# Two closing stages made one block, the chosen expert found inside the node stage, and the first four expert tiles taken singly

## What is computed

```python
H = gelu(layernorm(x) @ W1 + b1)              # 6250 x 1024
probs = softmax(H @ Wg + bg)                  # 6250 x 8
assign = argmax(probs)                        # the first largest
out = x + probs[assign] * (H @ Wd[assign] + bd[assign])
```

## Time and profile before

| | us |
|---|---|
| median of three runs | 2440.83 |
| the profiled execution | 2438.15 |
| its span in the trace | 2436.4 |
| busy: PE / DVE / POOL / ACT | 1969.0 / 1799.0 / 1456.7 / 869.7 |
| TensorE's mean granted clock | 0.902 |

### The profile page before, as it was taken

How to read it: one execution, slowest core, us unless ns; L and a number is a source line. 1 busy time by engine, 2 the same in 40 slices (tenths; PEclk the granted TensorE clock), 3 DMA queues, 4 the chain that set the end, 5 groups by cost and what they waited for, 6 DMA issues and landing times. The chain is left out here.

```text
span 2436.4 us, 50363 instructions
## 1 busy us (share of the span) xinstructions
PE 1969.0 (81%) x11356; PEld 1408.1 (58%) x11357; DVE 1799.0 (74%) x3100; ACT 869.7 (36%) x2796; POOL 1456.7 (60%) x1360
## 2 busy tenths in 40 slices
PE   8965777776777777777757999999889999679996
PEld 4533444554554544444545777777655555468885
DVE  6877999999999999999967888878776764321111
ACT  4532111111111111111116777777445555432221
POOL 4655777777777777777732777777654542023442
PEclk9987888888888888888878999999899999889998
DMA  6658999999999999999996888888534643464450
GB/s 218 222 177 275 359 362 358 361 360 354 360 362 355 363 356 359 358 358 360 349 231 205 304 277 278 280 278 277 170 130 169 219 159 119 172 232 168 154 186 36
DMA packets 388111, 649.78 MB, mean 267 GB/s; under 512 B 40235, under 2 KB 235951, under 8 KB 387925
## 3 DMA queue, kind: packets, MB, share of 16 engines
q1 hardware_dynamic: 200132, 277.43, 34.7%
q0 software_dynamic: 77824, 262.55, 30.2%
q10 hardware_dynamic: 110096, 109.07, 12.8%
HBM read 471.00 MB, written 178.83 MB: 267 GB/s over the span
## 5 line engine op out<-in xcount | busy, mean ns | idle before, releaser
L721 POOL DMA_INDIRECT s_kv<-kv_d,s_index x832 | 791.3, 951 | 266.0 <-issue 238.0
L1362 PE MATMUL a_sum_ps<-a_w,a_is_dst 128*128 128x260 f32 x1760 | 403.6, 388 | 20.5 <-DVE sums L1333 11.9
L1275 POOL TENSOR_TENSOR a_w<-a_v,a_w 128x512 f32<-128x512 f32 x220 | 299.1, 1365 | 164.8 <-ACT a_w L1232 107.5
L1362 PEld LDWEIGHTS a_sum_ps<-a_w,a_is_dst 128*128 128x128 f32 x1760 | 328.2, 191 | 95.8 <-issue 25.1
L867 PE MATMUL s_q_ps<-q,s_is_dst 128*128 x2496 | 366.9, 304 | 10.0 <-DVE s_key L776 8.7
L820 PE MATMUL s_mv_ps<-s_mixed 128*128 128x128 f32 x416 | 106.4, 436 | 272.2 <-DVE s_mixed L756 272.2
L771 DVE TENSOR_TENSOR s_key<-s_kv,s_rel_ps 128x1024 f32<-128x1024 f32 x208 | 253.3, 1218 | 63.0 <-issue 36.4
L867 PEld LDWEIGHTS s_q_ps<-q,s_is_dst 128*128 128x128 bf16 x2496 | 253.3, 107 | 79.2 <-issue 12.7
L1248 ACT ACTIVATE a_w<-a_v,a_w 128x64 f32<-128x64 f32 x1100 | 285.8, 335 | 3.5 <-DMA a_v<-v_d 3.5
L1309 DVE SCALAR_TENSOR_TENSOR a_is_dst<-node_of,first_node,a_col_ps 128x256 f32<-128x256 f32 x440 | 208.8, 475 | 82.7 <-PE a_sum_ps L1362 64.9
L781 DVE TENSOR_REDUCE s_part<-s_key 128x16 f32<-128x1024 f32 x208 | 253.7, 1220 | 10.7
(11 more groups left out here) (310 smaller groups left out, 2941.4 us busy)
## 6 DMA issues: line engine op xcount, KB each, us to landing
a_v<-v_d SPq DMA_DIRECT2D x440, 256.0 KB, 3.7
v_d<-s_kv ACTq DMA_DIRECT2D x208, 512.0 KB
s_local<-local_d SPq DMA_DIRECT2D x106, 256.0 KB, 6.0
xh_d<-h_hid SPq DMA_DIRECT2D x24, 1024.0 KB, 7.5
s_kind<-type_d SPq DMA_DIRECT2D x212, 64.0 KB, 6.6
s_kv<-kv_d,s_index POOLq DMA_INDIRECT x832
kv_d<-pkv SPq DMA_DIRECT2D x50, 256.0 KB, 2.0
wd<-in_L_ffn_Wd SPq DMA_DIRECT2D x8, 1024.0 KB, 12.0
```

The lines of the kernel that those rows point to most:

```text
L721: nc.gpsimd.indirect_dma_start(out=kv[:, g * GROUP + b, :], out_offset=None, in_=R["kv"], in_offset=bass.IndirectOffsetOnAxis(ap=index[:, ...
L1275: nc.gpsimd.tensor_tensor(heads(w[:, at, mine, 0:C]), heads(v[:, g, mine, :]), w[:, at, mine, C:, None].broadcast_to([P, len(tiles), H, D] ...
L1362: ins = nc.tensor.matmul(sum_ps[(g * PAIRS + k) % BANKS][:], is_dst[:, g % WRING, 2 * k + u, :], w[:, g % WRING, 2 * k + u, :], start=(u = ...
```

## The change

- In the node stage `read_logits(q)` now goes on, on DVE: the largest of the group's eight logits, the difference to it (written over `logits`), the first place of a zero, and `is_exp`. Five small instructions for each group (six for the last), each waiting for the one before. Five further small ones in step 0 prepare constants.
- SP no longer waits at the node stage's end. The semaphores of what follows are cleared by POOL at the end of its node program (29 instructions).
- Route and experts are one block, `stage_tail`, without a block of clears ahead of either. PE, whose first instructions are the two counting matmuls, waits for nothing there. SP, ACT, DVE and POOL first wait for the stored rows.
- `is_exp`, the counts and the places are laid out block by block instead of expert by expert. The scans read the counts from PSUM, without a copy.
- The sum and reciprocal of the probabilities move between the first chunk's first and second table.
- The first four gathers have a semaphore each (`opening`), and PE turns and multiplies the first four tiles one by one; the transposes of turn 1 follow the third and the fourth product.
- The tables of the route lie in the tiles of the experts (`e_xh`, `e_ht`, and their PSUM).

The diff, cut to its core:

```diff
@@ stage_nodes, sync @@
-            for w in range(2):
-                sp.wait_ge(stored[w], 16 * ((NQ + 1 - w) // 2))
-                sp.wait_ge(hid_out[w], 16 * NQ)
@@ stage_nodes, gpsimd, at its end @@
+            for sem in (*tail["route"].values(), *tail["experts"].values(), *tail["opening"], *tail["gathered"], *tail["scattered"]):
+                pool.sem_clear(sem)
@@ stage_nodes, vector, read_logits @@
+                dve.wait_ge(S["z_read"], q + 1)
...
+                then_pick(nc.vector.tensor_reduce(largest[:, 0:n], mine, AX_X, ALU.max))
+                then_pick(nc.vector.tensor_tensor(mine, mine, over(largest), ALU.subtract))
+                then_pick(nc.vector.scalar_tensor_tensor(out=choice[:, 0:n, :], in0=mine, scalar=0.0, in1=row(below_8),
+                                                         op0=ALU.is_equal, op1=ALU.mult))
+                then_pick(nc.vector.tensor_reduce(first[:, 0:n], choice[:, 0:n, :], AX_X, ALU.min))
+                then_pick(nc.vector.scalar_tensor_tensor(out=M["is_exp"][:, at, :], in0=over(first), scalar=float(NEXP),
+                                                         in1=row(M["col"]), op0=ALU.add, op1=ALU.is_equal))
@@ stage_tail, vector @@
-            then(nc.vector.tensor_copy(each[:], total_ps[:]))
             for e in range(NEXP):
-                st.mark(nc.vector.tensor_tensor_scan(running[:, e, 1:], M["ones"][:, 0:RBLK], each[:, e, :], 0.0,
+                st.mark(nc.vector.tensor_tensor_scan(running[:, 1:, e], M["ones"][:, 0:RBLK], by_block(total_ps)[:, :, e], 0.0,
...
+                if lo == 0:
+                    dve.wait_ge(S["exp_done"], 1)
+                    then(nc.vector.tensor_reduce(total[:], prob[:], AX_X, ALU.add))
+                    nc.vector.reciprocal(value[:, 1, :], total[:]).then_inc(S["chosen"], 1)
@@ stage_tail, tensor @@
+            regs = load_row(pe, at_expert, expert[0:1, 0:QUAD], NEXP - 1)
+            turn_tile(0)
+            turn_tile(1)
+            pe.wait_ge(S["wd_in"], 16 * NEXP)
+            for b in range(QUAD):
+                pe.wait_ge(X["copied"], 2 * b + 2)
+                product(0, b, regs)
+                if b + 2 < QUAD:
+                    turn_tile(b + 2)
+                else:
+                    if b == 2:
+                        pe.wait_ge(gathered[1], got(1))
+                    turn(1, range(4 * (b - 2), 4 * (b - 2) + 4))
```

More of the change, by code:

```diff
@@ L1875, in stage_route @@
+        perm_ps = t_ps[3][:, 0:2 * NTILE]
+        perm = perm_ps.rearrange("p (k t) -> p k t", t=NTILE)
+        wd, bd = M["wd"], M["bd"]
+        stored, hid_out = M["nodes"]["stored"], M["nodes"]["hid_out"]
+        S, X = M["tail"]["route"], M["tail"]["experts"]
+        opening, gathered, scattered = (M["tail"][n] for n in ("opening", "gathered", "scattered"))
         CHUNK = 7
         chunks = range(0, RBLK, CHUNK)
[L1877 to L1882, removed]
+        TURNS = NTILE // QUAD
@@ L1904, in _ @@
+            pool.wait_ge(S["near_set"], 2)
+            for n in range(XRING):
+                gather(n)
+            for n in range(TURNS):
+                if n + XRING < TURNS:
+                    pool.wait_ge(X["res_done"], (n + 1) * QUAD)
+                    gather(n + XRING)
+                scatter(n)
+            for w in range(2):
+                pool.wait_ge(scattered[w], 16 * QUAD * (TURNS // 2))
         @block.scalar
         def _(act):
-            act.wait_ge(S["shifted"], 1)
@@ L1932, in _ @@
-            dve.wait_ge(S["fixed"], 3)
-            dve.wait_ge(S["below_set"], 1)
-            st.mark(nc.vector.tensor_copy(ones_b[:], M["ones"][:]))
-            nc.vector.tensor_copy(below_b[:], below[:]).then_inc(S["halves_set"], 1)
-            st.settle()
-            then(nc.vector.scalar_tensor_tensor(out=choice[:], in0=choice[:], scalar=-float(NEXP), in1=by_expert(number),
-                                                op0=ALU.mult, op1=ALU.add))
-            st.mark(nc.vector.tensor_scalar(beyond[:], node[:, RBLK - 1:RBLK], float(N), None, ALU.is_ge))
@@ L1949, in _ @@
-            dve.wait_ge(S["exp_done"], 1)
-            then(nc.vector.tensor_reduce(total[:], prob[:], AX_X, ALU.add))
-            st.mark(nc.vector.tensor_scalar(value[:, 0, :], node[:, 0:RBLK], 1.0, None, ALU.add))
-            nc.vector.reciprocal(value[:, 1, :], total[:]).then_inc(S["chosen"], 1)
-            st.mark(nc.vector.memset(running[:, :, 0:1], 0.0))
+            rows_stored(dve)
+            st.mark(nc.vector.memset(running[:, 0, :], 0.0))
+            st.mark(nc.vector.memset(first_tile[:, 0:1], 0.0))
@@ L2007, in _ @@
+            st.mark(nc.vector.tensor_copy(weight[:], perm[:, 1, :]))
             st.settle()
[L2008 to L2012 removed]
@@ new lines, in product @@
+            def product(n, b, regs):
+                for c in range(HC):
+                    ins = nc.tensor.matmul(y_ps[n % 2][:, b, :], ht[:, n % 2, c, b * P:(b + 1) * P],
+                                           wd[:, bass.ds(regs[b], 1), c, :].rearrange("p a n -> p (a n)"),
+                                           start=(c == 0), stop=(c == HC - 1))
+                ins.then_inc(X["y_done"], 1)
+            at_expert = [pe.alloc_register(f"e_pe{b}") for b in range(QUAD)]
+            pe.wait_ge(S["expert_ready"], 1)
@@ L2205, in build @@
                 stage_aggregate(nc, A, M, R)
+            tail = lambda name: ctx.enter_context(nc.semaphore(name))
+            M["tail"] = {"route": {n: tail("r_" + n) for n in ROUTE_SEMS.split()},
+                         "experts": {n: tail("e_" + n) for n in EXPERT_SEMS.split()},
+                         "opening": [tail(f"e_opening{b}") for b in range(QUAD)],
+                         "gathered": [tail(f"e_gathered{r}") for r in range(XRING)],
+                         "scattered": [tail(f"e_scattered{w}") for w in range(2)]}
             stage_nodes(nc, A, M, R)
```

348 lines of the change are left out of this document (161 added, 187 removed).

## The result

The changed kernel takes **2446.48 us** (median of 20 runs, 2441.47 to 2452.28) against 2441.28 of the kernel before beside it (20 runs, 2439.09 to 2443.65). The ratio is 1.0020, with a 95% interval from 1.0014 to 1.0026: slower by 3.4 to 6.3 us. The direction was forecast and the time lies in the range, but of the rise of 11 only 5.2 came. The changed kernel also spreads over 10.8 us where the one before spreads over 4.6.

The account below looks back on a forecast made before the run. PE bounds the node stage, latency the tail. Stalls 18.6, seventh step 1.2 and clock 5.4, less the tail's 13.8, give +11.4 on 2438.15; with 2.7 from profiled execution to median, 2452 us, range 2432 to 2461.

Parts of the forecast that it names:

- The tail: From last logits to turn 1: forecast to gain 13.8 us (8.9 + 4.9), between 11 and 16.
- The path to the first gather: Tail, last logits to first gather: gather at 2138.5 instead of 2147.39, gain 8.9 us.
- The opening: Tail, first gather to first product of turn 1: 31.0 against 35.85 us, gain 4.9, between 3.5 and 6.5.
- The tail gives less: Rival: barrier, PSUM scans or gathers meeting weights' loads take back 3 to 5 us, 2456; chance 0.06 on top of stalls.
- single tiles wait anyway: Rival, opening: single tiles wait for all four gathers, so its 4.9 is lost, 2457; no separate chance given.
- Who comes first, and what follows: Node stage: POOL's L1500 precedes DVE's sums, DVE waits twice, n_v at 8.0, PE stalls 3.0 to 3.3 us.
- 3.1, in each of six steps: 18.6: Node stage: PE's stall for n_v per step, six steps concerned; bounds for a step 0.8 and 3.4 us.
- 1.2 for the seventh: Node stage, seventh step, already late before the change: the picks add 1.2 us there.
- 1.28 at the latest: Node stage: latest start of POOL's L1500 after the logits' read; DVE's first sum was put at 1.3.
- in all six: Node stage: DVE's first sum falls behind POOL's L1500 in every one of the six steps concerned.
- a mixed outcome: Node stage: some steps have POOL second; each step changing sides worth 2 us, with its clock 3; no separate chance.
- The clock: Node stage: PE's clock falls behind three of six stalls, 1.8 us each, 5.4; bounds 0 and 10.8.
- The sum by that rule: Whole kernel: clock falls only after a fully idle stretch, so no stall costs clock; 5.4 less, rise 6.0 us.

Follow-up runs that it names:

- e5: e1 with turn 0 put back: PE waits for all four gathers, turns all, then multiplies; 2692.13 us, ratio 0.9968 to the kernel before.
- e1: Changed kernel with the five picks one step later, in DVE's idle stretch behind the copy of l_ps; 2429.16 us, ratio 0.9944 to the kernel before.
- e2: Kernel before plus only the five picks behind read_logits, written to tiles nobody reads; 2460.82 us, ratio 1.0076 to the kernel before.
- e3: Changed kernel with POOL's x + beta moved behind its v * none, picks left in place; 2429.93 us, ratio 0.9950 to the kernel before.
- e6: e1 with all picks moved behind the node stage, as six operations in the tail; 2689.54 us, ratio 0.9955 to the kernel before.
- after: The changed kernel itself, first profile, against the kernel before; median 2446.48 us, ratio 1.0020.
- after_again: The changed kernel run once more unaltered, second profile; 2445.04 us, ratio 1.0013 to the kernel before.
- e4: Changed kernel with twelve identity transposes on PE before its wait for n_v in six steps; 2703.07 us, ratio 1.0013 to the kernel before.
- e10_idle_again: Same kernel as e1, run again on another chip as yardstick; ratio 0.9963 to the kernel before.

## Why the prediction was right, and where it was off

- **The tail, 13.8 forecast, 14.4 measured.** The path to the first gather won 9.5 instead of 8.9; each station came within 0.7. The opening won the 4.9 forecast, but by two errors that cancel: the first landing, taken at 5.2, came at 7.0 and moved the first product from 9.5 to 10.5, and this product took 3.95 instead of the 4.9 allowed. "The tail gives less" and "single tiles wait anyway" fall; e5 measures the tiles at 7.
- **Who comes first, and what follows.** POOL ahead of `sums`, `n_v` at 8.0, a wait of PE of 3.1: measured 7.7 to 8.0 and 2.7 to 3.0, in five of six steps and then in four of six. (PE begins 2.7 to 3.0 after the 5.04 at which it was due; the rows call 2.6 to 2.9 of this a wait.) e1, e2 and e3 show the place of the picks and POOL's two sums as the cause. The Trainium skill (SBUF — State Buffer, the section on who interferes with whom) says that a VectorE instruction with two SBUF inputs contends with a GpSimd instruction that reads SBUF, and that one with at most one SBUF input, outside the two-port modes, doesn't. The traces agree: the picks that were held (2.30, 2.29, 1.55 and 2.14 in the fences) subtract or compare two tensors, while the reductions kept 0.16 to 0.19 in every profile, also in the midst of a sum of POOL's. The prediction applied this to the large sums only and put five picks at 0.22 apart.
- **The step that failed: "3.1, in each of six steps: 18.6", and 1.2 for the seventh.** The mechanism was right and its size wrong: in place of the 18.6 the trace has 12.0, and in place of the 19.8 of all seven 12.7. A stall is not all loss. Before, PE waited 0.38 for ACT's copy to `h_hid` between the halves of the `n_v` transposes, and from their start (1893.47) to the next matmul 1.47 passed:

```profile
1894.45 0.66 PE L1722 MATMUL n_swap_ps<-ident,n_v 128*128 128x128 f32 x4 [0.38 <-ACT h_hid L1540]
1894.94 1.88 PE L1761 MATMUL h_h_ps<-n_x2t,h_w 128*128 128x512 f32 x4
```

Behind a stall it is 0.93 (1902.85 to 1903.78). So 0.54 come back in each of the six, 3.2. One step escaped and was 0.9 late, 2.2 less. The five others were 2.9 late on average, 1.1 less in all, and the seventh lost 0.7 instead of 1.2.
- **Why one step escaped.** "1.28 at the latest" for POOL's first sum came from six steps of one trace and was taken for a limit. It is none: the sum begins up to 1.76 after the read in the first profile of the changed kernel, 2.61 in the second, and 2.10 in e6, whose steps have no picks. So "in all six" rested on too few rows, and a mixed outcome was given no chance of its own.
- **The clock, 5.4 forecast, 6.8 measured** (four gaps by 1.7, and 278.42 - 271.66 in PE's busy time); in the second profile three. Over the profiles of after, after_again and e2 it fell behind 10 of 14 gaps of 2.6 to 2.9 us. By the rule of the Trainium skill that the prediction weighed (TensorE: Matmul & The Clock Gate, What's actually happening) it would have fallen behind none. The sum by that rule, a rise of 6.0, lies nearer to the 5.2 measured, but that is luck: the clock did cost 6.8. e4, which leaves only 1.3 to 1.6 of the gap empty, keeps the clock in all six steps, so the cause is the gap. What tells the ten from the four stays open.
- Sum for the node stage: 25.2 - 3.2 - 2.2 - 1.1 - 0.5 + 1.4 = 19.6, measured 19.7. With the tail that is +5.3 instead of +11.4.
- Also missed: that which steps escape can differ from execution to execution. The first step, which lasted 30.27 in the first profile and 27.04 in the second, makes the 2.8 between the two (19.7 and 16.9); all others together differ by 0.4 the other way. That such steps make the whole spread of the changed kernel is likely, but not shown.

## What to carry to other kernels

Count a small instruction by what it may be held behind, not by its size: on an engine that another one can lock out, five operations of 0.2 us ahead of a critical one cost 3 us and more. Work that nobody waits for belongs where its engine is idle and where the next consumer is far, and a few lines of reordering decided here between 5 us lost and 14 us won. When a stall is counted, subtract the small waits that it swallows.

## What the hardware showed beyond that

- An indirect gather that is issued while 1 MB and the last of 8 MB of plain loads are on the way lands after 7.0 and 7.2 us (after, e1_idle_place); with the 1 MB held back, or issued 3.3 us later, after 4.7. That the loads are the cause fits all of these, but the loads were never taken away altogether. The wait moved, the time hardly did.
- The same kernel takes 10% more on another chip (2698 against 2444), nearly all of it ahead of the first group's logits, which are read at 2104.7 instead of 1843.8 (e10_idle_again and e1_idle_place, one kernel), while the usual step of 26.27 and the turn of 18.39 are the same on both to 0.01. A sum of stretches from the trace could still resolve 1 us there, where the runs resolved 5.
